# Rounding the FFN weights on VectorE alone, and a third batch's context transposed in blocks

## What is computed

```python
def reference(x, ctx_2048, mask_BxS2_bk0, g_xattn, g_ffn, L0_ffn_w_gating, L0_ffn_w_linear):
    x = x + jnp.tanh(g_xattn[0]) * _L0_xattn_ref(_layernorm(x, axis=-1), ctx_2048, mask_BxS2_bk0)
    x = x + jnp.tanh(g_ffn[0]) * _L0_ffn_ref(_layernorm(x, axis=-1), L0_ffn_w_gating, L0_ffn_w_linear)
    return x
...
def _L0_xattn_ref(hidden_states, memory_tokens, memory_mask):
    scores = jnp.einsum('bsd,bmd->bsm', hidden_states, memory_tokens) * scale
    scores = jnp.where(memory_mask[:, None, :], scores, neg_inf)
    attn = jax.nn.softmax(scores, axis=-1)
    readout = jnp.einsum('bsm,bmd->bsd', attn, memory_tokens)
...
def _qdot(x, w, out_dtype=BF16):
    return jnp.dot(x.astype(E4M3), w.astype(E4M3), preferred_element_type=out_dtype)
...
    gate_value = jax.nn.gelu(_qdot(x, w_gating[0]))
    activations = gate_value * _qdot(x, w_gating[1])
    outputs = _qdot(activations, w_linear)
```

## Time and profile before

| | |
|---|---|
| median of 3 runs | 134.54 us (133.6 to 134.76) |
| profiled execution | 132.98 us |
| its span | 131.2 us |
| granted TensorE clock | 1.0 of full speed (the 2.4 GHz level) in every stretch |
| PE / PE weight load busy | 92% / 79% |
| DVE / ACT / POOL busy | 68% / 69% / 71% |

### The profile page before, as it was taken

How to read it: one execution, slowest core, us unless ns; L and a number is a source line. 1 busy time by engine, 2 the same in 40 slices (tenths; PEclk the granted TensorE clock), 3 DMA queues, 4 the chain that set the end, 5 groups by cost and what they waited for, 6 DMA issues and landing times.

```text
span 131.2 us, 2509 instructions
## 1 busy us (share of the span) xinstructions
PE 120.9 (92%) x846; PEld 103.1 (79%) x846; DVE 89.1 (68%) x187; ACT 90.8 (69%) x141; POOL 93.2 (71%) x90
## 2 busy tenths in 40 slices
PE   6849999999799999899999899999999959999991
PEld 4438978989789998779999599999987955454780
DVE  1347479989996874998673984394694665767852
ACT  3189999699978893979665680599672876947300
POOL 3069930579999899999999999999989833930000
PEclk9999999999999999999999999999999999999999
DMA  1697999699992997503600069015000000000035
GB/s 44 195 383 229 397 233 261 105 179 188 296 254 102 182 179 126 179 1 85 235 5 0 12 180 308 5 12 148 0 0 7 2 0 0 0 0 5 0 124 196
DMA packets 33908, 15.93 MB, mean 121 GB/s; under 512 B 25700, under 2 KB 32616, under 8 KB 33896
## 3 DMA queue, kind: packets, MB, share of 16 engines
q1 hardware_dynamic: 33608, 15.77, 46.4%
q10 hardware_dynamic: 288, 0.00, 0.1%
HBM read 14.72 MB, written 1.05 MB: 120 GB/s over the span
## 4 chain that ended last, share of the span: by engine, by line
PE 37%; POOL 35%; ACT 8%; DVE 6%; issue 5%; DMA 5%; SPq 1%; POOLq 0%; DVEq 0%; ACTq 0%
POOL ws L436 7%; POOL cTl_a L430 7%; PE scores L774 7%; PE pv L750 6%; POOL wq L437 6%; POOL chl_a L422 5%; PE ring L790 5%; DMA xs<-in_x_dram 5%; PE ring L719 5%; PE pv L754 3%; PE scores L736 3%; PE scores L732 3%; PE scores L737 3%; POOL chl_b L422 2%; POOL cTl_b L430 2%
## 5 line engine op out<-in xcount | busy, mean ns | idle before, releaser
L481 ACT ACTIVATE pT_hi<-ring 128x512 fp32r<-128x512 f32 (+1 forms) x32 | 15.3, 508 | 8.7 <-PE pv L754 4.5
L422 POOL TENSOR_TENSOR chl_a<-cn,chl_a 128x1024 fp32r<-128x1024 f32 x8 | 19.2, 2399 | 1.9 <-ACT chl_a L496 1.9
L599 DVE TENSOR_TENSOR pT_lo<-ring,pT_hi 128x512 fp32r<-128x512 f32 (+1 forms) x32 | 17.8, 578 | 3.3 <-ACT pT_hi L481 3.3
L750 PE MATMUL pv<-chl_a,pT_hi 128*128 128x256 f32 x128 | 18.6, 287 | 0.1
L617 DVE CUSTOM_DVE_ANT_0 sp<-scores,bias 128x1024 f32<-128x1024 f32 (+1 forms) x16 | 15.6, 983 | 4.1 <-PE scores L737 1.9
L422 POOL TENSOR_TENSOR chl_b<-cn,chl_b 128x1024 fp32r<-128x1024 f32 (+1 forms) x8 | 12.5, 1569 | 7.3 <-ACT chl_b L496 6.8
L719 PE MATMUL ring<-ident,sp 128*128 128x128 f32 (+1 forms) x104 | 16.0, 273 | 1.2 <-DVE cTl_b L599 0.7
L750 PEld LDWEIGHTS pv<-chl_a,pT_hi 128*128 128x128 f32 x128 | 16.4, 189 | 0.6 <-DVE xs L636 0.3
L516 ACT ACTIVATE sp<-sp,nb,sc 128x1601 f32<-128x1601 f32 x8 | 13.8, 1724 | 3.5 <-DVE nb L624 3.5
L750 PE MATMUL pv<-chl_b,pT_hi 128*128 128x256 f32 (+1 forms) x80 | 12.8, 291 | 2.2 <-ACT pT_hi L481 1.3
L436 POOL TENSOR_TENSOR ws<-ws,wg 128x1024 f32<-128x1024 f32 x6 | 14.3, 2390 | 0.6 <-DVE wg L641 0.6
(11 more groups left out here) (80 smaller groups left out, 278.0 us busy)
## 6 DMA issues: line engine op xcount, KB each, us to landing
cn<-in_ctx_dram SPq DMA_DIRECT2D x12, 512.0 KB, 4.8
cb<-in_ctx_dram SPq DMA_DIRECT2D x16, 192.0 KB, 3.7
ws<-in_L_ffn_w_gating_dram SPq DMA_DIRECT2D x4, 512.0 KB, 5.4
ws<-in_L_ffn_w_linear_dram SPq DMA_DIRECT2D x2, 512.0 KB, 4.5
out_dram<-xs SPq DMA_DIRECT2D x8, 128.0 KB, 1.8
mrow<-in_mask_BxS_bk_dram SPq DMA_DIRECT2D x4, 200.1 KB, 6.0
xs<-in_x_dram SPq DMA_DIRECT2D x2, 256.0 KB, 5.4
xs<-in_x_dram SPq DMA_DIRECT2D x1, 512.0 KB, 5.1
```

Source lines behind the costliest of these rows:

```text
L422: nc.gpsimd.tensor_tensor(chl(b, g)[0:parts, :, D:2 * D], cn[0:parts, t0:t1, :], chl(b, g)[0:parts, :, 0:D].bitcast(f32), ALU.subtract).th ...
L481: nc.scalar.activation(dst, bank_view(f, size), ACT.Copy, scale=-1.0 if f[0] == "X" else 1.0).then_inc(hi_ready, 1)
L599: nc.vector.tensor_tensor(dst, bank_view(f, size), hi.bitcast(f32), ALU.subtract).then_inc(freed, 1)
L750: nc.tensor.matmul(pv[:, 0:D], pT_hi[0:parts, t, :], ctx[0:parts, t - t0, D * part:D * (part + 1)], start=(t == 0 and part == 0), stop=False)
```

## The change

Four things are changed, and all five order texts are written anew.

1. DVE alone rounds a piece: `w_round` has two instructions with two SBUF inputs each, both with the maximum inside. POOL's `round_w` and its steps `I` are gone. The second instruction gives the negative of the rounded weight; GELU takes its input with scale -1, and the signs of the second and third product cancel. SP's loads and ACT's |w| wait for DVE's step.
2. `BLOCKED` has batch 1 too: `C1:0` to `C1:5` are gone, `b1` and `D1:0` to `D1:2` are new. The context of batch 1 is loaded with 1 KB rows, and its bias is one instruction in place of two.
3. x of batch 0 is loaded, measured, scaled, centred and transposed tile by tile (`XPART`): steps `G`, `F`, `K`, `X` 0 and 1 are a tile each, 2 to 4 a batch each. `G3` and `G4` wait for one load of both batches.
4. The mask of batch 0 is loaded first and its bias made first.

```diff
+    XPART = [(0, 1), (1, 2), (2, 4), (4, 6), (6, 8)]
...
-    BLOCKED = (2, 3)
+    BLOCKED = (1, 2, 3)
...
     SP_ORDER = steps("""
-        x0 c0:0 x1 c0:1 c0:3 c0:2 m1 m0 c1:0 x2 c1:1 w0 m2 c1:2 b2 c1:3 c2:0 w1 m3 c2:1 w2 b3 c2:3 w3 c3:1 c2:2
...
+        m0 c0:1 x0 c0:0 x1 c0:2 x2 c0:3 b1 c1:3 x3 c1:0 c1:1 m1 m2 c1:2 w0 w1 b2 c2:3 m3 c2:0 w2 c2:1 b3 c2:2
...
                 if i >= 2:
-                    sp_eng.wait_ge(w_ready, pool_i[("I", i - 2)])
+                    sp_eng.wait_ge(w_ready, dve_w[("W", i - 2)])
...
-            def round_w(i):
-
-                pool.wait_ge(wg_ready, dve_w[("W", i)])
-                link(nc.gpsimd.tensor_tensor(ws[:, i % 2, :], ws[:, i % 2, :], wg[:, :], ALU.add))
-                nc.gpsimd.tensor_tensor(wq[:, i, :], ws[:, i % 2, :], wg[:, :], ALU.subtract).then_inc(w_ready, 1)
...
                 if i >= 1:
-                    actor.wait_ge(w_ready, pool_i[("I", i - 1)])
+                    actor.wait_ge(w_ready, dve_w[("W", i - 1)])
...
-                                     ACT.Gelu_apprx_tanh).then_inc(gate_ready, 1)
+                                     ACT.Gelu_apprx_tanh, scale=-1.0).then_inc(gate_ready, 1)
...
-            def w_grid(i):
+            def w_round(i):
+
                 dve.wait_ge(abs_ready, act_w[("W", i)])
-                nc.vector.tensor_scalar(wg[:, :], wg[:, :], GRID_MIN * 2.0 ** 20, None, ALU.max).then_inc(wg_ready, 1)
+                link(nc.vector.scalar_tensor_tensor(out=ws[:, i % 2, :], in0=wg[:, :], scalar=GRID_MIN * 2.0 ** 20,
+                                                    in1=ws[:, i % 2, :], op0=ALU.max, op1=ALU.add))
+                nc.vector.scalar_tensor_tensor(out=wq[:, i, :], in0=wg[:, :], scalar=GRID_MIN * 2.0 ** 20,
+                                               in1=ws[:, i % 2, :], op0=ALU.max, op1=ALU.subtract).then_inc(w_ready, 1)
...
-                    todo = [(bank[:, (KD * q + k) * P:(KD * q + k + 1) * P], xc[:, QT * f[1] + q, k * P:(k + 1) * P], P)
-                            for q in range(QT) for k in range(KD)]
+                    j0, j1 = XPART[f[1]]
+                    todo = [(bank[:, (KD * i + k) * P:(KD * i + k + 1) * P], xc[:, j0 + i, k * P:(k + 1) * P], P)
+                            for i in range(j1 - j0) for k in range(KD)]
```

More of the change, by code:

```diff
@@ L102, in gated_cross_attention_ffn @@
-        H10 H11 H12 H13 H14 H15 Y1 Y2 Y3 Y4 Y5 Y6 Y7""")
+        C0:2 C0:3 X0 C0:1 C0:0 S0:1 C0:5 X1 C0:4 S0:0 C0:6 S0:2 S0:3 X2 S1:0 S1:1 T0:0 T0:1 S1:2 T0:2 S1:3 T0:3
+        V0:0 C1:6 V0:1 V0:2 V0:3 T1:3 T1:1 T1:0 S2:0 T1:2 S2:1 V1:0 S2:3 S2:2 V1:1 V1:2 X3 T2:0 T2:1 V1:3 S3:1
+        T2:3 T2:2 S3:2 X4 S3:0 S3:3 V2:0 C2:6 V2:1 V2:2 V2:3 T3:0 T3:2 S4:0 S4:1 T3:1 S4:3 S4:2 T3:3 V3:0 S5:0
+        V3:1 T4:0 T4:1 T4:2 S5:1 V3:2 V3:3 N0 T4:3 S5:3 S5:2 V4:0 S6:0 V4:1 V4:2 T5:1 C3:6 V4:3 S6:1 T5:3 T5:0
@@ L104, in counted @@
+        S6:3 S6:2 T5:2 V5:0 V5:1 S7:1 T6:1 S7:2 T6:0 N1 S7:0 T6:2 T6:3 V5:2 V5:3 S7:3 V6:0 V6:1 H0 T7:0 T7:3
+        V6:2 T7:1 V6:3 T7:2 H1 V7:0 V7:1 V7:2 N2 V7:3 H2 H3 H4 H5 H6 N3 H7 H8 H9 H10 H11 Y0 H12 H13 H14 H15 Y1
+        Y2 Y3 Y4 Y5 Y6 Y7""")
     def counted(order, letters):
@@ L118, in gated_cross_attention_ffn, with xpart @@
     act_b = counted(ACT_ORDER, "B")
-    pool_z, pool_d, pool_i = (counted(POOL_ORDER, c) for c in "ZDI")
+    pool_z, pool_d = (counted(POOL_ORDER, c) for c in "ZD")
     fills = [s for s in PE_ORDER if s[0] in "XCTN"]
     turns = [s for s in DVE_ORDER if s[0] == "D"]
+    def xpart(j):
+        return next(i for i, (a, z) in enumerate(XPART) if a <= j < z)
     def scored_by(j, *cs):
@@ L204, in pair @@
             return (hbanks[i], None) if i < 2 else (hbanks[(i - 2) % 3], None if i == 4 else i - 2 if i < 4 else i - 3)
-        x_in = [sem(f"x_in{i}") for i in range(3)]
+        x_in = [sem(f"x_in{i}") for i in range(4)]
         g_in = sem("g_in")
@@ L320, in load_x @@
             def load_x(i):
-                a, z = QT * i, J if i == 2 else QT * (i + 1)
+                a, z = XPART[i][0], J if i == 3 else XPART[i][1]
                 sp_eng.dma_start(xs[:, a:z, :], x_v[:, a:z, :]).then_inc(x_in[i], 16)
@@ L463, in gates, with centre @@
                 nc.scalar.activation(tg[:], graw[:], ACT.Tanh).then_inc(tg_ready, 1)
-            def centre(b):
-                actor.wait_ge(mean_ready, dve_g[("G", b)])
-                for j in range(QT * b, QT * (b + 1)):
+            def centre(i):
+                actor.wait_ge(mean_ready, dve_g[("G", i)])
+                for j in range(*XPART[i]):
                     ins = nc.scalar.activation(xc[:, j, :], xs[:, j, :], ACT.Identity, bias=mv[:, j, 0:1], scale=-1.0)
@@ L472, in fill_hi @@
                 if f[0] == "X":
-                    if f[1] >= 2:
-                        actor.wait_ge(scored, max(scored_by(j, 0, 1, 2, 3) for j in range(QT * (f[1] - 2), QT * (f[1] - 1))))
+                    b = XPART[f[1]][0] // QT
+                    if b >= 2:
+                        actor.wait_ge(scored, max(scored_by(j, 0, 1, 2, 3) for j in range(QT * (b - 2), QT * (b - 1))))
                 elif f[0] == "C":
@@ L657, in _ @@
                 if s[0] == "G":
-                    dve.wait_ge(x_in[min(s[1], 2)], 16)
-                    stats(range(QT * s[1], QT * (s[1] + 1)), st, mv, mean_ready)
+                    dve.wait_ge(x_in[min(s[1], 3)], 16)
+                    stats(range(*XPART[s[1]]), st, mv, mean_ready)
                 elif s[0] in "XCT":
@@ L673, in _ @@
                 elif s[0] == "W":
-                    w_grid(s[1])
+                    w_round(s[1])
                 elif s[0] == "H":
@@ L759, in hidden @@
                 if i == 0:
-                    pe.wait_ge(w_ready, max(pool_i[("I", k)] for k in range(4)))
+                    pe.wait_ge(w_ready, max(dve_w[("W", k)] for k in range(4)))
                 if i % HT == 0:
```

57 lines of the change are left out of this document (24 added, 33 removed).

## The result

| | median | profiled execution | its span |
|---|---|---|---|
| before (20 runs) | 133.4 us | 132.98 us | 131.2 us |
| changed (20 runs) | 134.68 us | 135.1 us | 133.1 us |

The changed kernel takes 1.0093 times the time of the one before, with a 95% interval of 1.0067 to 1.0119: slower by about 1.2 us, where 4.8 us less were forecast. The measured time lies outside the range of 127.5 to 133.7 us. (Ratios here leave out disturbed executions; "before" got 17 more runs than stood ahead of the prediction, and its median went from 134.54 to 133.4 us with them.)

What follows compares the result with a forecast made beforehand. PE, busy 92% of the span, was taken as the bound, with its start and few waits. Terms -2.6 - 2.0 + 0 - 2.0 + 1.8 = -4.8 us gave 128.2 us profiled, 129.7 us as median; range 127.5 to 133.7.

Steps and rivals of the forecast that it cites:

- DVE with the rounding: DVE's six weight pieces, two instructions each: 0.3 us a piece uncovered, +1.8 us, from 0 to +15.6.
- rival (a): DVE's two-input rounding meets POOL's SBUF work; three of six pieces held twice, 135.7 us; chance 0.10 in full.
- So one wait is mostly covered, two are not: DVE's rounding pieces: PE's already fed work mostly hides one wait of up to 2.4 us for POOL, not two.
- The start, -2.0: Tile 0: bias made first, its sp transposes start at 19.5 instead of 21.64 us; -2.0 us, from 0 to -2.8.
- the transposes, -2.6: PE: the 24 transposes of C1:0 to C1:5 go, 6 x 0.43 us, -2.6 us.
- A first score later than 12 us: Start of the kernel: a sign that would make the forecast wrong; the first score was expected at about 10.7 us.
- POOL without the rounding, -2.0: POOL from 37 us on: busy 93.2 to about 72 us, PE's waits go; -2.0 us, from 0 to -2.5.
- Relief on POOL alone is worth no more than PE's waits: From 57 to 95 us: PE has only 0.60 us less than full, so POOL's queue is just in time.
- Batch 1 in blocks: Batch 1's block loads, turns and rests ready for tile 2's scores: nothing in sum, from -0.7 to +3 us.
- rival (b): Batch 1's block loads land at 25 rather than 20 us: +2 to 3 us, 132.2 us; chance 0.16 with mild (a).
- The end: Near 106 us: PE's wait of 1.32 us at 106.72 goes, leaving under 0.5 us.
- The carry-over: Whole kernel: the profiled execution's 1.56 us under its median carries over, from 128.2 us profiled to 129.7 us.

Runs made afterwards that it cites:

- the version with the ACT copy: Changed kernel with one ACT copy a piece converting the weights to 8 bits, |w| and DVE's two rounding instructions gone: 128.28 us, ratio 0.9634.
- the one with transposes: Changed kernel with the twelve DVE rounding instructions replaced by 32x32 block transposes of the same size, FFN weights left at zero: 128.35 us, ratio 0.9624.
- the rounding's part alone: Kernel before with DVE rounding in two instructions at the old places, POOL's two instructions gone, all else as before: 137.17 us, ratio 1.0203.
- the longer warm-up: Changed kernel with 42 instead of 22 warm-up matmuls: 134.91 us, ratio 1.0063.

## Why the prediction was wrong

The failing step is the size of the term "DVE with the rounding": +1.8 us in the sum, 0.3 us a piece, within bounds of 0 to +15.6. The runs show 6.3 us in its place. The mechanism was in the prediction, as rival (a) with its page, and it holds; what it costs was judged by how long DVE alone would be held and by a cover counted piece by piece. Measured:

- **The meeting**: 6.3 us (128.35 against 134.68), on top of a free price that costs nothing measurable (the version with the ACT copy is as fast as the one with transposes, with 16.6 us less of DVE busy time). Behind W1 I gave DVE a cover of 4.6 us, the four V of tile 2. In the trace these V had ended at 52.44 us, before the piece began at 52.94, and what covered it were one fill and the wide scores of tile 4, until 56.52. The piece took 6.03 us. The next fill, T3:1, needs the bank of C2:6, because the ring has three banks, and C2:6's `cTl_b` stands behind W1 in DVE's order. The cover ends at the first fill whose bank is freed behind the piece, not at the last V.
- **I priced one side only.** POOL was held for 9.4 us too. TensorE's wait of 0.95 us that ends at 81.41 us is for a cTl_a subtraction that lasted 3.45 us in place of 2.40, beside a piece (W2) whose own instructions took 1.22 and 1.23. No term of the sum had this.
- **"So one wait is mostly covered, two are not"**: only one piece had both waits, W1, and only one other had one, W3, with 4.49 us. Moving W1 alone was worth 2.5 us (1.0093 to 0.9903). So rival (a), at 135.7 us, came near the measured time partly by luck: it took three pieces held twice on DVE, and there was one, with POOL's side of the cost left out.

**The start, -2.0, and the transposes, -2.6.** Together 4.6 us; everything but the rounding measured 1.3 to 1.4 together, and no run takes the two apart. By the rows, the sum counted work twice: tile 0's first transposes of sp were to come 2 us earlier partly because C1:0, C1:1 and C1:3, 1.3 us of PE, no longer stand ahead of them, and these are among the 24 of the other term. The earlier trace rows had said that the stretch up to 21.6 us had 1.05 us of idle to give. And the start itself came out late: the first transpose at 8.31 us instead of 7.66, the first score at 12.53 and not 10.7, tile 0's first transposes of sp at 22.25 and not 19.5 (the kernel before: 21.64). A first score later than 12 us was one of the prediction's own signs of being wrong. With transposes in place of the rounding, tile 0's first transposes of sp come at 21.56 us in the new order and at 21.54 in the old one: the start as a whole gave nothing there, with 1.3 us of PE work less ahead of it and part of the new start at half rate.

**POOL without the rounding, -2.0.** Right in kind and too small: 3.6 us with DVE's free pieces in it. I took PE's named waits as all that POOL could give (0.7 and 1.32 us). "Relief on POOL alone is worth no more than PE's waits" is the sentence that failed. The page's chain had put 35% of the span on POOL. By the profiles, TensorE's idle between its first transpose and its last matmul falls from 4.8 to 2.7 us and its busy time by 1.0; the rest of the 3.6 us isn't placed.

**Batch 1 in blocks** cost no wait, as the sum had it, but at other times than forecast. The eight loads were issued from 6.48 to 18.90 us. The first turn came at 24.81 us (21.5 forecast) and the first rest ended at 29.64 (26.5); tile 2's first score came at 31.02 (28). Both sides were 3 us late, and TensorE has no wait between 21.6 and 36.5 us. That both shifted alike is luck. DVE had no wait for the block loads, so rival (b), late loads, has nothing for it.

**The end**: the wait of 1.32 us near 106 us is gone, as forecast; TensorE is busy 15.78 of 16.00 us from 95 to 111.

**The carry-over.** The step of 1.56 us from the profiled execution to the median came from three runs; with 20 runs it is 0.42 us. This moves the forecast in microseconds by 1.1 and its difference to the kernel before by nothing.

With the measured sizes the sum is -3.6 (POOL's relief and DVE's free pieces) - 1.4 (everything else) + 6.3 (the meeting) = +1.3 us, and 1.2 were measured. For the changed kernel this closes by construction, since the three sizes are differences between it, its variants and the kernel before. The kernel before tests it: -3.6 + 6.3 = +2.7 us, and the rounding's part alone measured +2.7 (1.6 to 3.8).

## What to carry to other kernels

Where DVE and POOL both work on SBUF, look in the trace for DVE instructions with one form and two durations; where they exist, an instruction with two SBUF inputs moved from POOL to DVE is to be priced as an exchange of turns, on both engines, and its cheap form is one that the trace shows with a single duration beside POOL's work, as the block transpose here. A single SBUF input is no guarantee: L641 has one, and it met POOL. Two dependent instructions can be held twice, as W1 was, when the other engine's next instruction goes between them. And before two gains are added, hold their sum against the idle of the stretch: a saving that shows as an earlier landmark and one that shows as work removed can be the same microseconds.

## What the runs showed of the hardware

- A 128x1024 DVE instruction with two f32 SBUF inputs takes 1.19 to 1.25 us free, for f32 and for bf16 output alike, and 2.09 to 3.43 when it meets a POOL subtraction of 2.4 us. With one SBUF input, a 128x1024 tensor_scalar (L641) takes 0.68 to 0.69 us free and 2.15 to 2.53 when it meets one, while a block transpose of this size beside the same subtractions always takes 1.20 to 1.25.
- POOL is held as well: 128x2 steps of 0.19 us took 1.18 and 1.20, a 128x1 step of 0.39 us took 1.43 (at 76.42 us), and a subtraction of 2.40 us took 3.45.
- In the changed kernel's profile the first eight transposes take 1.94 us and the pair of matmuls behind the next eight 1.20, against 1.06 and 0.71 with the longer warm-up, while the granted clock of that stretch reads 1.00 in both. In the version with the copy the same start reads 0.76 from 7.66 to 21.6 us, between the 2.4 GHz and the 1.2 GHz level; there the first eight take 1.06, and the next eight 1.92. TensorE had been idle 2.4 and 2.5 us before them. In the kernel before and its variants with the same start the first eight took 1.06 us after 1.62 and 1.75 us of idle, and 1.94 after 1.83 and 2.67 us. So the same start can fall on either side, and the reading of the clock doesn't always show it.
